# Adding the experts' output biases in the attention's projection, once per batch

## The chip, the cores and the metric

The kernel runs on one core of a Trainium2 chip. Its time is the device time of one execution in microseconds, the median of several runs. The engines of the core are TensorE (PE in the profile, with PEld for its weight loads), VectorE (DVE), ScalarE (ACT), GpSimd (POOL) and SyncE (SP), which here only issues DMAs.

## What is computed

Two layers on 16 x 256 tokens of width 128. Cut to what matters here:

```python
# layer 0
xn = layernorm(x)
attn = causal_linear_attention(xn) @ Wo.T              # 16 heads of 8
probs = softmax(xn @ Wg + bg)                          # 8 experts
selected = top2(probs) / (sum of the two + 1e-8)       # the gates
h = gelu(einsum('bsf,efh->bseh', xn, W1) + b1)
expert_out = einsum('bseh,ehf->bsef', h, W2) + b2      # b2: 8 x 128
x = x + attn + einsum('bsef,bse->bsf', expert_out, selected)
# layer 1
xn = layernorm(x)
x = x + (linear_attention(xn) @ w_proj + b_proj) + channel_mix(xn)
```

## The kernel before

The 4096 tokens lie in 32 tiles of 128; two tiles are a batch, four a group (8 groups). The stages, in the order of time:

- **First stage (to about 33 us).** For each group g: DVE takes the moments, POOL the deviation, ACT `normalise(g)` (L306) writes xn, PE transposes it (L335), ACT copies the transpose (L378), PE projects to values (L352) and queries and keys (L364), DVE multiplies by cosine and sine (L393). Four xn buffers take turns, so `normalise(4)` may only overwrite xn[0] once SP's DMA `save(0)` (L1281) has put it into DRAM. In ACT's order it is: values copy of g, xT copy of g+1, `normalise(g+2)`.
- **Routing (to about 58 us).** DVE picks two experts for each token, and the tokens are sorted by expert into 71 slots of 128 rows. Small products on PE and idle fillers (`keep_warm`, L320) run beside it.
- **Expert stage (to about 270 us).** PE's program is a fixed list of steps, one for each slot j: transpose the gathered tokens of slot j+2 (L545), `up` of slot j+1 (four f32 products, two records each, L561), what the list puts between, and `down` of slot j (L572 and L574). Between them stand the attention's parts: 32 cumulative sums (L700, L701; one every 2 slots or a little more), and for each batch two transposes (L746) and the projection (L776). PE executes strictly in this order. DVE does the elementwise part of the attention: tile (b, r) is apply (L712), outer (L667), sums (L721), and after r = 1 reciprocal, divide (L734), low part (L684) and phi (L642). ACT does gelu, copies and the high parts (L678). POOL gathers tokens and expert rows.
- **Second layer (to the end).** Linear attention and channel mix, group by group, the tokens' last additions done by DVE.

Before the change the bias b2 enters at each slot. It is split into three bf16 parts (POOL, L401 to L409), which six DMAs of SP (L1304) lay into three rows of `bias3`, zero elsewhere; a product of an all-ones matrix with the expert's 128 columns (L572) opens each `down`, with the column picked by a register. b_proj is added in the same manner (L1055, L1139).

SP's program order around the change is: loads of x, weights, `bg` (L1272), b2 (L1273), b_proj (L1274), mu (L1275, L1276), then `save(0)`, `save(1)`, two weight loads, then save and w2 loads in turn. A DMA waits in this queue for all that stand ahead of it.

```python
        if g >= NB:
            if layer == 0:
                act.wait_ge(xT_ps, g - NB + 2)
                act.wait_ge(xn_saved[n], g // NB * 16)
```

Of the kernel before, what the change touches and what calls it, by code (L numbers as in the profile page):

```python
# [22 lines left out]
BIASP, NBIAS = NE * D, NE * D + D  # L23
# [4 lines left out]
for _name, _n in (("ident", P), ("head_mask", P + H), ("cos", 2 * DH), ("sin", 2 * DH), ("first", NE),  # L28
                  ("row_no", 1), ("rows_in_front", 1), ("token_by_tile", NT),
                  ("ones", P), ("tri_incl", P), ("tri_excl", P), ("iota", P), ("token", NT * TOPK)):  # L30
    CONSTS[_name] = (_at, _at + _n)
    _at += _n
# [3 lines left out]
def constant_table():  # L36
# [21 lines left out]
    put("row_no", row)  # L58
    put("rows_in_front", P * row)
# [6 lines left out]
def build(nc, x_in, Wq, Wk, Wv, Wo, Wg, bg, W1, b1, W2, b2, w_qkv, w_proj, b_proj, W_r, W_k, W_v,  # L66
# [33 lines left out]
    xn = [sbuf(f"xn{p}", [P, GT, D]) for p in range(NB)]  # L100
# [18 lines left out]
    bias_sp = sbuf("bias_sp", [P, NBIAS // P])  # L119
    bias_rest = sbuf("bias_rest", [P, 2, NBIAS // P])  # L120
    bias_part = sbuf("bias_part", [P, 3, NBIAS // P], bf16)
    bias3 = sbuf("bias3", [P, NBIAS], bf16)
# [97 lines left out]
    y_tok, yT0 = sbuf("y_tok", [P, 2 * D])[:, :], sbuf("yT0", [P, 2 * P])[:, :]  # L220

# [9 lines left out]
    bias_in, bias_split, bias_rows = sem("bias_in"), sem("bias_split"), sem("bias_rows")  # L231
    small_ready, pool_const, warmed, bias_zero = sem("small_ready"), sem("pool_const"), sem("warmed"), sem("bias_zero")
# [164 lines left out]
    def split_biases(pool):  # L397


        pool.wait_ge(bias_in, 16 * 5)  # L400
        nc.gpsimd.tensor_copy(bias_part[:, 0, :], bias_sp[:, :]).then_inc(bias_split, 1)  # L401
        pool.wait_ge(bias_split, 1)
        nc.gpsimd.tensor_tensor(bias_rest[:, 0, :], bias_sp[:, :], bias_part[:, 0, :], ALU.subtract).then_inc(bias_split, 1)
        pool.wait_ge(bias_split, 2)
        nc.gpsimd.tensor_copy(bias_part[:, 1, :], bias_rest[:, 0, :]).then_inc(bias_split, 1)
        pool.wait_ge(bias_split, 3)
        nc.gpsimd.tensor_tensor(bias_rest[:, 1, :], bias_rest[:, 0, :], bias_part[:, 1, :], ALU.subtract).then_inc(bias_split, 1)
        pool.wait_ge(bias_split, 4)
        nc.gpsimd.tensor_copy(bias_part[:, 2, :], bias_rest[:, 1, :]).then_inc(bias_split, 1)  # L409
# [155 lines left out]
    def down(pe, base, s, e):  # L565
        j, p = slot(base, s), s % 2
        pe.wait_ge(gelu_ready, j + 1)
        if not from_(j, 1):
            pe.wait_ge(w2_in, 16 * NE)
            pe.wait_ge(bias_rows, 16 * 6)  # L570
# [169 lines left out]
    Y_COLS = slice(P, 3 * P)  # L740

    def attn_transpose(pe, b):

        pe.wait_ge(y_ready, b + 1)
        for t in range(2):
# [3 lines left out]
    def attn_yT(act, b):  # L749
# [3 lines left out]
        nc.scalar.copy(yT0, ps[6][:, Y_COLS]).then_inc(yT_ready, 1)  # L753
# [17 lines left out]
    def attn_project(pe, b):  # L771

        pe.wait_ge(tokens_put, b + 1)
        pe.wait_ge(yT_ready, b + 1)
        for t in range(2):
# [345 lines left out]
    def last_tensor(pe):  # L1121
# [16 lines left out]
        for h in range(2):  # L1138
            nc.tensor.matmul(out_half(h), ones_bf[:, :], bias3[:, BIASP:BIASP + D].unsqueeze(1).broadcast_to([P, HALF, D]),  # L1139
# [113 lines left out]
    with nc.Block() as block:  # L1253
        @block.sync
        def _(sp):
# [17 lines left out]
            sp.dma_start(bias_sp[:, 0:BIASP // P], b2.rearrange("e h -> (e h)").rearrange("(p c) -> p c", p=P)).then_inc(bias_in, 16)  # L1273
# [522 lines left out]
```

## Time and profile before

| | |
|---|---|
| median of 3 runs | 354.57 us (354.26 to 354.77) |
| the profiled execution | 354.33 us |
| its span, first to last instruction | 352.5 us |
| mean granted TensorE clock | 0.995 |
| instructions | 9136 |

Times of the views are microseconds from the start of the span. The span is 1.8 us shorter than the execution's own time. Records of PE overlap: a product's duration includes its drain, and its price in a dense stream is the distance to the next start. PEclk is the granted clock in tenths of full speed.

### The profile page before, as it was taken

The page shows a single profiled execution, that of the slowest core. Times are in us where ns is not written, and L with a number is a line of the kernel's source. Part 1 is how long each engine was busy: PE and PEld are TensorE (multiplying, and loading weights), DVE is VectorE, ACT ScalarE, POOL GpSimd, SP SyncE. Part 2 cuts the span into 40 slices and gives each one's busy share as a digit, 9 for nine tenths or more (in the row PEclk, how much of TensorE's full clock was granted, in tenths as well). Part 3 has the DMA queues.
Part 4 walks back from the last instruction along what each step waited for, and adds up shares of the span by engine and source line. Part 5 has one row for each costly group of instructions (what it writes and reads, how often), then busy time and mean ns, then how long its engine had stood idle before and what let it go on. Part 6 is the DMA issues. An engine that isn't in the chain of part 4 may idle for free.

```text
span 352.5 us, 9136 instructions
## 1 busy us (share of the span) xinstructions
PE 339.4 (96%) x2488; PEld 296.4 (84%) x2488; DVE 320.9 (91%) x633; ACT 271.4 (77%) x764; POOL 208.8 (59%) x229
## 2 busy tenths in 40 slices
PE   8999878999999999999999999999999899999995
PEld 3888334799999999999999899999998688778875
DVE  5999999899999999998899899998978799998665
ACT  2997946968887878787787678778985987777751
POOL 3899202843323666766776678778877278884110
PEclk9999989999999999999999999999999999999999
DMA  5896196454444555555555654565452002221112
GB/s 161 238 278 181 32 387 240 114 147 131 136 130 137 156 152 149 159 150 156 155 157 154 168 155 133 164 186 145 120 141 75 9 7 54 60 63 30 30 32 60
DMA packets 45520, 46.98 MB, mean 133 GB/s; under 512 B 6928, under 2 KB 33712, under 8 KB 45216
## 3 DMA queue, kind: packets, MB, share of 16 engines
q1 hardware_dynamic: 40432, 37.17, 35.7%
q0 software_dynamic: 4320, 8.86, 10.1%
q10 hardware_dynamic: 720, 0.38, 0.5%
q8 instruction: 22, 0.36, 0.5%
q14 instruction: 26, 0.21, 0.2%
HBM read 32.88 MB, written 13.50 MB: 132 GB/s over the span
## 4 chain that ended last, share of the span: by engine, by line
PE 86%; DVE 9%; DMA 2%; issue 2%; POOL 0%; ACT 0%; DVEq 0%; POOLq 0%
PE banks L574 18%; PE banks L561 18%; PE banks L700 7%; PE banks L701 7%; PE banks L364 4%; PE banks L1012 3%; PE banks L545 3%; PE banks L1041 2%; PE banks L1088 2%; PE banks L352 2%; PE banks L1070 2%; PE banks L1050 2%; PE banks L776 2%; PE banks L1022 2%; PE banks L1058 2%; PE banks L320 2%
## 5 line engine op out<-in xcount | busy, mean ns | idle before, releaser
L489 POOL DMA_INDIRECT xg<-xn_rows,slot_tok x71 | 76.5, 1077 | 77.0 <-PE banks L545 43.6
L591 ACT ACTIVATE xT<-banks,b1T 128x128 f32<-128x128 f32 x284 | 81.5, 375 | 18.8 <-PE banks L561 18.6
L506 POOL DMA_INDIRECT qk_exp<-expert_rows,ranki x64 | 74.0, 1156 | 19.1 <-issue 18.7
L574 PE MATMUL banks<-w_sb,xT 128*128 x568 | 78.9, 282 | 0.0
L561 PE MATMUL banks<-xgT,w 128*128 128x128 f32 x568 | 75.4, 276 | 0.0
L574 PEld LDWEIGHTS banks<-w_sb,xT 128*128 128x128 f32 x568 | 69.3, 192 | 0.5
L561 PEld LDWEIGHTS banks<-xgT,w 128*128 128x128 f32 x568 | 69.0, 192 | 0.8 <-issue 0.5
L712 DVE TENSOR_TENSOR cq<-banks,phi 128x360 f32<-128x360 f32 (+1 forms) x96 | 47.4, 548 | 7.6 <-PE banks L701 6.7
L684 DVE TENSOR_TENSOR low<-outer,high 128x1152 fp32r<-128x1152 f32 x32 | 43.5, 1358 | 3.2 <-ACT high L678 3.2
L721 DVE TENSOR_REDUCE sums<-cq 128x144 f32<-128x1152 f32 x32 | 43.0, 1343 | 0.1
L678 ACT CAST high<-outer 128x1152 fp32r<-128x1152 f32 x32 | 36.9, 1154 | 7.0 <-DVE outer L667 5.7
L667 DVE TENSOR_TENSOR outer<-phi,qkv 128x1024 f32<-128x1024 f32 x32 | 38.8, 1215 | 0.0
L700 PE MATMUL banks<-high,tri_r 128*128 128x360 f32 (+1 forms) x96 | 35.0, 365 | 0.0
L701 PE MATMUL banks<-low,tri_r 128*128 128x360 f32 (+1 forms) x96 | 32.3, 337 | 0.0
L600 ACT COPY ye<-banks 128x128 f32<-128x128 f32 x71 | 18.8, 265 | 13.0 <-PE banks L574 12.5
L320 PE MATMUL banks<-zeros_bf 128*128 128x512 bf16 x96 | 27.2, 427 | 1.0 <-DVE zeros_bf L1555 1.0
L306 ACT ACTIVATE xn<-x_sb,shift,rstd 128x128 f32<-128x128 f32 x60 | 24.9, 485 | 0.1
L963 POOL TENSOR_TENSOR outer<-outer,x_sb 128x512 f32<-128x512 f32 x7 | 8.9, 1276 | 22.0 <-DVE outer L958 22.0
L545 PE MATMUL banks<-cst,xg 128*128 128x128 f32 x71 | 19.6, 276 | 1.3 <-issue 0.5
L583 ACT COPY xgT<-banks 128x128 f32<-128x128 f32 x71 | 19.4, 273 | 0.8
L320 PEld LDWEIGHTS banks<-zeros_bf 128*128 128x128 bf16 x96 | 10.0, 111 | 11.6 <-issue 4.4
L287 POOL TENSOR_TENSOR rstd<-ve,mhalf 128x4 f32<-128x4 f32 x16 | 18.8, 1173 | 1.3
(210 smaller groups left out, 691.0 us busy)
## 6 DMA issues: line engine op xcount, KB each, us to landing
w<-in_L_ffn_W SPq DMA_DIRECT2D x71, 256.0 KB
expert_rows<-ye SPq DMA_DIRECT2D x71, 64.0 KB
expert_rows<-x_sb SPq DMA_DIRECT2D x2, 2048.0 KB, 9.7
x_sb<-in_L_attn_x SPq DMA_DIRECT2D x8, 256.0 KB, 4.0
xn_rows<-xn SPq DMA_DIRECT2D x8, 256.0 KB, 2.9
w_sb<-in_L_ffn_W SPq DMA_DIRECT2D x8, 256.0 KB, 3.9
out<-outer SPq DMA_DIRECT2D x7, 256.0 KB, 2.4
xg<-xn_rows,slot_tok POOLq DMA_INDIRECT x71
```

The costliest lines, as they stand in the source:

```text
L320: nc.tensor.matmul(ps[bank], zeros_bf[:, :], zeros_bf[:, :].unsqueeze(1).broadcast_to([P, 4, P]), start=True, stop=True)
L489: pool.indirect_dma_start(out=xg[n][:, :], out_offset=None, in_=xn_dram, in_offset=bass.IndirectOffsetOnAxis(ap=slot_tok[:, j:j + 1], axis ...
L506: pool.indirect_dma_start(out=y_moe[:, i, k, :], out_offset=None, in_=y_dram, in_offset=bass.IndirectOffsetOnAxis(ap=ranki[:, 0, k, i:i + ...
L561: last = nc.tensor.matmul(slot_bank(j)[:, c * P:(c + 1) * P], w1[n][:, c * P:(c + 1) * P], xgT[p][:, :], start=True, stop=True)
L574: last = nc.tensor.matmul(y, hidT[p][:, c, :], w2_sb[:, ds(e * NC + c, 1), :], start=False, stop=(c == NC - 1))
L591: last = nc.scalar.activation(hidT[p][:, c, :], slot_bank(j)[:, c * P:(c + 1) * P], ACT.Gelu_apprx_tanh, bias=b1T[:, ds(e * NC + c, 1)])
L667: nc.vector.tensor_tensor(outer_of(r)[:, :, 0:DH, :], k.unsqueeze(2).broadcast_to([P, H, DH, DH]), vv.unsqueeze(3).broadcast_to([P, H, DH, ...
L684: nc.vector.tensor_tensor(low[n], outer[r], high[n].bitcast(f32), ALU.subtract).then_inc(low_ready, 1)
L700: nc.tensor.matmul(o, w[:, :], high[at][:, cols], start=(m == 0), stop=False)
L701: last = nc.tensor.matmul(o, w[:, :], low[at][:, cols], start=False, stop=(m == len(parts) - 1))
L712: last = nc.vector.tensor_tensor(cq4[:, lo:hi, :, :], ps[n][:, 0:(hi - lo) * E9 * DH].rearrange("p (h e d) -> p h e d", e=E9, d=DH), q[:, ...
L721: nc.vector.tensor_reduce(sums[:, r, :, :], cq4, AX.X, ALU.add).then_inc(sums_ready, 1)
```

## The change

The sum over a token's two experts of gate times bias is a product of the token's eight gates (zero for the others) with the 8 x 128 matrix b2. The changed kernel adds it on PE where a batch's attention is projected, accumulated in the same PSUM bank: one fp32r product for each batch of two tiles, with 64 contraction rows and 256 columns. The 64 rows are the 16 gates (two tiles of eight experts) in a high and a low part, against the bias in a high and a low part. The product of each slot (L572) goes.

What it needs: the bias matrix in 128 rows, loaded by 16 small DMAs of b2 (8 rows each) and two of b_proj (1 row each) on SP's queue, behind the mu loads and ahead of the saves, after a wait for a memset; its parts by one operation on ACT and one on POOL in place of POOL's five and SP's six bias DMAs; the gates of all tokens by expert, from DVE operations in the routing and in `gates`; `split_gates` on DVE after tile (0, 1), two operations of 512 columns, the second of which waits for the first; one transpose on PE for every second batch, in front of the attention's own, where the first waits for `split_gates`; and one copy on ACT for each of them. b_proj uses the new matrix with an fp32r product.

```diff
-        nc.tensor.matmul(y, ones_bf[:, :], bias3[:, ds(e * D, D)], start=True, stop=False)
         for c in range(NC):
             last = nc.tensor.matmul(y, hidT[p][:, c, :], w2_sb[:, ds(e * NC + c, 1), :],
-                                    start=False, stop=(c == NC - 1))
+                                    start=(c == 0), stop=(c == NC - 1))
...
     def attn_transpose(pe, b):
         pe.wait_ge(y_ready, b + 1)
+        if b == 0:
+            pe.wait_ge(gates_split, 1)
+        if b % 2 == 0:
+            nc.tensor.transpose(ps[6][:, 3 * P:4 * P], gate_row[:, b * NGR:(b + 2) * NGR], ident)
...
+        if b % 2 == 0:
+            nc.scalar.copy(gT[:, :], ps[6][:, 3 * P:4 * P])
+        nc.scalar.copy(yT0, ps[6][:, P:3 * P]).then_inc(yT_ready, 1)
...
         for t in range(2):
-            last = nc.tensor.matmul(ps[5][:, t * D:(t + 1) * D], yT0[:, t * P:(t + 1) * P], wT[:, 0, :],
-                                    start=False, stop=True, skip_group_check=True)
-        last.then_inc(o_ps, 1)
+            nc.tensor.matmul(ps[5][:, t * D:(t + 1) * D], yT0[:, t * P:(t + 1) * P], wT[:, 0, :],
+                             start=False, stop=False, skip_group_check=True)
+        rows = slice(b % 2 * NGR, (b % 2 + 1) * NGR)
+        nc.tensor.matmul(ps[5][:, 0:2 * D], gT[rows, :], bias[rows, 0:2 * D], start=False, stop=True,
+                         skip_group_check=True).then_inc(o_ps, 1)
...
-        nc.tensor.matmul(ps[4], ones_bf[:, :], bias3[:, BIASP:BIASP + D].unsqueeze(1).broadcast_to([P, GT, D]),
+        nc.tensor.matmul(ps[4], ones_r[:, :], bias[:, BIASP:NBIAS].unsqueeze(1).broadcast_to([P, GT, D]),
...
-            sp.dma_start(bias_sp[:, 0:BIASP // P], b2.rearrange("e h -> (e h)").rearrange("(p c) -> p c", p=P)).then_inc(bias_in, 16)
-            sp.dma_start(bias_sp[:, BIASP // P:NBIAS // P], b_proj.rearrange("(p c) -> p c", p=P)).then_inc(bias_in, 16)
             sp.dma_start(mu[:, 0:1], mu_r.rearrange("(p c) -> p c", p=P)).then_inc(bias_in, 16)
             sp.dma_start(mu[:, 1:2], mu_k.rearrange("(p c) -> p c", p=P)).then_inc(bias_in, 16)
+
+            sp.wait_ge(zeros_ready, 2)
+            for q in range(P // (2 * NE)):
+                for t in range(2):
+                    lo = (2 * q + t) * NE
+                    sp.dma_start(bias_raw[lo:lo + NE, t * D:(t + 1) * D], b2).then_inc(bias_loaded, 16)
+            for lo in (0, 32):
+                sp.dma_start(bias_raw[lo:lo + 1, BIASP:NBIAS], b_proj.rearrange("(a c) -> a c", a=1)
+                             ).then_inc(bias_loaded, 16)
...
+    def bias_high(act):
+        act.wait_ge(bias_loaded, 16 * 18)
+        nc.scalar.activation(bias_high_of, bias_raw, ACT.Copy, scale=const("low_row")).then_inc(bias_ready, 1)
+
+    def bias_parts(pool):
+        pool.wait_ge(bias_ready, 1)
+        nc.gpsimd.tensor_tensor(bias[:, :], bias_raw, bias_high_of.bitcast(f32), ALU.subtract).then_inc(bias_ready, 1)
...
+            both = TT(oh[:, 0, :, :], oh[:, 0, :, :], oh[:, 1, :, :], ALU.add)
...
+            done(TT(gate_of_all, masked, oh[:, 0, :, :], ALU.mult))
...
+                done(TT(gate_of_all, gate_of_all, sel[0][:, :].unsqueeze(2).broadcast_to([P, NT, NE]), ALU.mult))
+
+            def split_gates():
+                whole = yT0[:, 0:NT * NE].rearrange("p (b f) -> p b f", b=B).unsqueeze(2).broadcast_to([P, B, 2, 2 * NE])
+                done(nc.vector.tensor_copy(gate_parts[:, :, :, 0, :], whole))
+                TT(gate_parts[:, :, :, 1, :], whole, gate_parts[:, :, :, 0, :].bitcast(f32), ALU.subtract
+                   ).then_inc(gates_split, 1)
...
                     tile(b, r, b % 2)
+                    if b == 0 and r == 1:
+                        split_gates()
```

## Rows read from the trace of the kernel before

**Rows 1.** The page: busy us (share of the span), instructions.
```profile
PE 339.4 (96%) x2488; PEld 296.4 (84%) x2488; DVE 320.9 (91%) x633; ACT 271.4 (77%) x764; POOL 208.8 (59%) x229
```

**Rows 2.** Busy time by window: engines, granted clock, DMA share, GB/s.
```profile
20.00:30.00 10.00, 10.00 (x63) 8.55 (x62) 9.97 (x23) 8.87 (x25) 9.53 (x14) 1.00 0.80 236
40.00:50.00 10.00, 6.58 (x26) 2.78 (x27) 9.38 (x30) 5.77 (x7) 0.00 (x0) 0.84 0.70 248
150.00:160.00 10.00, 10.00 (x82) 9.58 (x81) 9.84 (x14) 8.40 (x28) 5.80 (x6) 1.00 0.52 154
```

**Rows 3.** The chain that ended last, expert stage: start us, us, what.
```profile
157.80 0.16 PE banks L700
...
158.71 0.20 PE banks L701
158.91 0.07 PE banks L572
158.98 0.95 PE banks L574 x8
...
160.03 0.89 PE banks L561 x8
```

**Rows 4.** DVE's timeline, waits for PE: start us, us, what, idle before.
```profile
166.39 1.49 DVE L712 TENSOR_TENSOR cq<-banks,phi 128x360 f32<-128x360 f32 x3 [0.78 <-PE banks L701]
...
265.70 1.49 DVE L712 TENSOR_TENSOR cq<-banks,phi 128x360 f32<-128x360 f32 x3 [2.98 <-PE banks L701]
```

**Rows 5.** ACT's timeline, first stage.
```profile
17.79 0.59 ACT L378 COPY xT<-banks 128x512 f32<-128x512 f32 x1
18.27 1.65 ACT L306 ACTIVATE xn<-x_sb,shift,rstd 128x128 f32<-128x128 f32 x4
...
21.44 1.65 ACT L306 ACTIVATE xn<-x_sb,shift,rstd 128x128 f32<-128x128 f32 x4
```

**Rows 6.** SP's timeline, then the issues of lines 1281 and 1304, ns.
```profile
13.30 0.44 SPq L1273 DMA_DIRECT2D bias_sp<-in_L_ffn_b  x1
...
15.21 0.98 SPq L1281 DMA_DIRECT2D xn_rows<-xn  x2
...
L1281 SPq DMA_DIRECT2D xn_rows<-xn x8: 366/442/584, 15.2 to 29.9; - x8
DMA to landing us min/median/max: 2.2/2.9/5.7
...
L1304 SPq DMA_DIRECT2D bias<-bias_part x6: 562/601/1467, 37.8 to 41.9; - x6
```

**Rows 7.** PE's timeline: the transposes of groups 4 and 6.
```profile
20.32 0.60 PE L335 MATMUL banks<-cst,xn 128*128 128x128 f32 x4
...
26.84 0.60 PE L335 MATMUL banks<-cst,xn 128*128 128x128 f32 x4
```

**Rows 8.** PE's one long gap, the chain behind it, and ACT's wait.
```profile
46.69 0.56 PE L472 MATMUL banks<-by_turn,ones_r 128*128 128x72 f32 x2 [3.42 <-DVE by_turn L1656]
...
47.25 2.56 PE banks L320 x6
...
49.91 0.28 ACT L1382 CAST slot_no<-banks 128x144 f16<-128x144 f32 x1 [4.13 <-PE banks L477]
```

**Rows 9.** DVE at phi(2), and the chain's piece of PE's first L746.
```profile
81.67 0.68 DVE L642 SCALAR_TENSOR_TENSOR phi<-qk_exp,qkv 128x512 f32<-128x512 f32 x1
82.28 1.48 DVE L712 TENSOR_TENSOR cq<-banks,phi 128x360 f32<-128x360 f32 x3
...
81.86 0.22 PE banks L746 x2
```

**Rows 10.** The chain's first product of line 574 behind line 572.
```profile
152.19 0.17 PE banks L574
```

**Rows 11.** PE's timeline around the 32-row transposition.
```profile
34.04 0.60 PE L1504 MATMUL banks<-cst,outer 128*128 128x128 f32 x4
34.57 0.24 PE L1505 MATMUL banks<-cst,outer 32*128 32x32 f32 x1
34.75 2.98 PE L320 MATMUL banks<-zeros_bf 128*128 128x512 bf16 x13
```

More of the change, by code:

```diff
@@ L22 @@
 BIG = 3.0e38
-BIASP, NBIAS = NE * D, NE * D + D
+BIASP, NBIAS = 2 * D, 3 * D
+NGR = 4 * 2 * NE
 CONSTS = {}
@@ L58, in constant_table @@
     put("row_no", row)
+    put("low_row", row // 32 % 2)
     put("rows_in_front", P * row)
@@ L99, in build @@
     NB = 4
-    xn = [sbuf(f"xn{p}", [P, GT, D]) for p in range(NB)]
+    xn_all = sbuf("xn_all", [P, NB, GT, D])
+    xn = [xn_all[:, p, :, :] for p in range(NB)]
     xT = [sbuf(f"xT{p}", [P, GT, P]) for p in range(2)]
@@ L118, in build @@
     bg_sb = sbuf("bg_sb", [P, NE])
[L119 to L122, printed above, removed]
+    bias = sbuf("bias", [P, NBIAS], f32r)
     ones_bf = sbuf("ones_bf", [P, P], bf16)
@@ L220, in build @@
     y_tok, yT0 = sbuf("y_tok", [P, 2 * D])[:, :], sbuf("yT0", [P, 2 * P])[:, :]
+    gT = sbuf("gT", [P, P], f32r)
+    bias_high_of = high[2][:, 0:NBIAS]
+    bias_raw = phi_all[:, 4 * D:4 * D + NBIAS]
+    gate_row = xn_all[:, 2:4, :, :].rearrange("p n c f -> p (n c f)")
+    gate_parts = gate_row.bitcast(f32r).rearrange("p (b c s f) -> p b c s f", b=B, c=2, s=2)
+    gate_of_all = yT0[:, 0:NT * NE].rearrange("p (a e) -> p a e", e=NE)
     ps_all = st.enter_context(nc.psum_tensor("banks", [P, 8 * 512], f32))
@@ L1138, in last_tensor @@
         for h in range(2):
-            nc.tensor.matmul(out_half(h), ones_bf[:, :], bias3[:, BIASP:BIASP + D].unsqueeze(1).broadcast_to([P, HALF, D]),
+            nc.tensor.matmul(out_half(h), ones_r[:, :], bias[:, BIASP:NBIAS].unsqueeze(1).broadcast_to([P, HALF, D]),
                              start=True, stop=False, skip_group_check=True)
@@ L1299, in _ @@
                 sp.wait_ge(x_loaded[g], 16)
-            sp.wait_ge(bias_split, 5)
-            sp.wait_ge(bias_zero, 1)
-            for n in range(3):
-                for lo, hi in ((0, BIASP), (BIASP, NBIAS)):
-                    sp.dma_start(bias3[n:n + 1, lo:hi].rearrange("a (p c) -> a p c", p=P),
-                                 bias_part[:, n, lo // P:hi // P]).then_inc(bias_rows, 16)
             rows = y_dram.rearrange("(p r) d -> p (r d)", p=P)
@@ L1377, in _ @@
             nc.scalar.copy(b1T[:, :], ps[1][:, 0:NE * NC]).then_inc(w_late_ready, 1)
+            bias_high(act)
             for g in range(1, NG - 2):
@@ L1428, in first @@
                 act.wait_ge(pool_const, 4)
+                act.wait_ge(bias_ready, 2)
                 nc.scalar.activation(scrap["scalar"], scrap["zero"], ACT.Gelu_apprx_tanh).then_inc(warmed, 1)
@@ L1457, in _ @@
                     deviation(pool, 0, g + 5, g + 5)
-            split_biases(pool)
+            bias_parts(pool)
             pool.wait_ge(logits_read, 1)
@@ L1555, in _ @@
             nc.vector.memset(zeros_bf[:, :], 0.0).then_inc(zeros_ready, 1)
-            nc.vector.memset(bias3[:, :], 0.0).then_inc(bias_zero, 1)
+            nc.vector.memset(bias_raw, 0.0).then_inc(zeros_ready, 1)
             nc.vector.memset(keep, 1.0).then_inc(route, 1)
@@ L1583, in choose @@
                 v.wait_ge(v_raw, NT // 2)
-                v.wait_ge(bias_in, 16 * 5)
+                v.wait_ge(bias_in, 16 * 3)
                 TT(lg, qkv3[:, :, 3 * D:NQ], per_expert(bg_sb[:, :]), ALU.add).then_inc(logits_read, 1)
@@ L1719, in _ @@
                 rope_sum_vector(v, NG - 1, f)
+            both = TT(oh[:, 0, :, :], oh[:, 0, :, :], oh[:, 1, :, :], ALU.add)
+            n_route[0] += 1
+            both.then_inc(route, 1)
             v.wait_ge(gate_exp, 1)
-            done(RED(row(5), masked, AX.X, ALU.add))
+            RED(row(5), masked, AX.X, ALU.add)
+            v.wait_ge(route, n_route[0])
+            done(TT(gate_of_all, masked, oh[:, 0, :, :], ALU.mult))
             def gates():
@@ L1747, in _ @@
             for b in range(2):
+                if b == 1:
+                    v.wait_ge(bias_ready, 2)
                 phi(v, b, b)
```

22 lines of the change are left out of this document (5 added, 17 removed).

## The prediction

> **What bounds the kernel now.** I read the page first. TensorE (PE) is busy in 96% of the span and VectorE (DVE) in 91% [rows 1], so neither share alone says which one sets the end. The windows say more. In the first stage (20 to 30 us) PE and DVE are both full; from 150 to 160 us, inside the expert stage, PE is full and DVE has 0.16 us of idle in ten [rows 2]. The chain that ended last, asked for a stretch of the expert stage, runs on PE alone [rows 3]: what PE issues there is on the path, and the pieces of the chain are the true price of an instruction (start to start), where its own duration includes a drain that the next one hides. The DVE timeline gives the second limit: its apply (L712) waited for PE in few places, the first large one 0.78 us at 166.39, the largest the last, 2.98 us at 265.70 [rows 4]; they lie where the schedule puts extra slots. So DVE follows PE closely, but it follows.
>
> The first stage has the same form. The chain there is PE's transposes and projections at 3.17 us for each group of four tiles, and ACT's order (values copy, xT copy, normalise) has the same period: normalise starts at 18.27 and at 21.44 us [rows 5]. SP is not busy in any table, but its queue issues loads back to back there [rows 6], and that is the part of the profile that decides this change.
>
> **The change on SP's queue.** 18 loads (16 copies of b2 by eight rows, two of b_proj) stand between the mu loads and the first save of xn. Two loads (L1273, L1274) go. Four issues from 13.30 to 15.21 us give 0.478 us each [rows 6]; so the first save moves by 16 x 0.478 = 7.6 us, from 15.21 to 22.8. The new wait in front of them, on a memset at DVE's start, is long over by 15 us and costs nothing. Who waits behind it: save(0) must land before normalise(4) may overwrite xn[0]. Its landing takes 2.2 at best, 2.9 us in the median [rows 6]. Today that is 17.4 to 18.1 us and normalise(4) starts at 18.27, as soon as ACT is free [rows 5]: the cover is under a microsecond. After: 22.8 + 2.2 to 2.9 = 25.0 to 25.7, so ACT stands for 6.7 to 7.4 us; I take 7.1. PE needs these tiles for the transposes at 20.32 [rows 7], 0.4 us behind ACT, and ACT, PE and DVE hold the rest of their work behind it. Nothing catches up, as PE and ACT both run at 3.17 us a group with no gap; only about 0.2 us comes back that PE lost to DVE between the transposes at 20.32 and 26.84, two groups in 6.52 us where 6.34 would do [rows 7]. Save(1) to save(3) follow at once and are in time. Bounds for one issue: 0.37 (the shortest save, 366 ns) to 0.6 (the median of L1304, 601 ns) [rows 6], that is 5.9 to 9.6 us for 16, and a stall of about 5.0 to 9.4.
>
> **The clock.** PE will then idle for some 6.8 us. The trace shows one such gap: PE waited 3.42 us for DVE (L472), and the six warm-up products behind it took 2.56 us on the chain (47.25 to 49.81), where 13 of the kind took 2.98 (0.22 each, 1.3 for six) [rows 8, 11]; the window's granted clock is 0.84, the lower level of 1.2 GHz for part of it [rows 2]. So a gap costs about 1.3 us in these rows and 0.2 in L472; I take 1.4, with 0 and 3 as bounds. It is on the path, because the work behind this gap is real.
>
> The Trainium skill (TensorE: Matmul & The Clock Gate, Why this matters for your kernels) warns against idle gaps of TensorE between bursts of products, since the clock falls behind them; the trace agrees, with the 0.84 just given.
>
> **SP and the others between 33 and 60 us.** The five Pool splits, the six bias DMAs (3.6 us by six medians of L1304 [rows 6]) and SP's wait for them go; the fill of expert_rows starts earlier. DVE's chain of routing sets the time there and none of this stands in it, so I count 0. ACT's bias_high (about 0.45 us, 384 columns, by the xT copy's 0.59 for 512 [rows 5]) lies in front of the 4.13 us that ACT idles before L1382 [rows 8]; Pool's subtraction, one in place of five, before its long wait for the slots. DVE's three or four extra routing operations come after the slot numbers have left, 256 columns each, some 0.4 us by phi's 0.68 for 512 [rows 9]; they delay phi and the first low part by some 0.7 us, and PE's first cumulative sum by about 0.5. That is absorbed by the next item.
>
> **A new wait of PE at the gates.** split_gates stands behind tile (0,1) and phi(2) on DVE, which end at 82.28 [rows 9]. It is two operations on 512 columns, one of which needs the other's end: 0.68 us each by phi (L642, 512 columns) [rows 9], so ready at about 83.7. PE's first transpose of the attention (L746) starts at 81.86 now [rows 9] and would wait in order, with up and down of the next slots behind it. With the gates' own transpose (0.11) L746 starts at 83.85: +1.95 us on PE, whatever it had saved before. DVE itself is 1.35 later and keeps its slack (the waits of [rows 4] are still ahead of it), so it doesn't become the bound.
>
> **What PE saves.** Per slot the bias product L572 costs 0.07 us of the chain behind a cumulative sum [rows 3] and little less elsewhere. The eight products behind it cost 0.95, where the eight of L561 cost 0.89 [rows 3]: the first of them takes 0.17, not 0.11 [rows 10], because its weights can't load behind so short a product. I take both as gone: 0.06 + 0.06 = 0.12 a slot. Behind the gates' wait 65 slots are left: 7.8 us (3.9 if only the product itself counts).
>
> **What PE gets.** Seven more transposes at 0.11 (two of L746 take 0.22 [rows 9]): 0.8 us. 16 products of 64 rows by 256 columns, fp32r: 360 columns cost 0.16 and 432 cost 0.20 [rows 3], so 0.12 for 256, or 1.9 us. But they use half of the array's rows. The trace has one operation on part of the rows, the transposition L1505 of 32 rows: it starts 0.20 us after the last of L1504 (34.57 against 34.04 + 3 x 0.11) and the product behind it 0.18 later, where whole-array neighbours are 0.11 and at most 0.11 apart [rows 11]. So entering and leaving costs 0.1 each: 0.32 a product, 5.1 us in all. Bounds: 0.12 (1.9 us) and 0.45, if both sides cost the full 0.165 by which one transposition exceeds its step (four of L1504 take 0.60, so one takes 0.27) (7.2 us). I take 5.1, because the 32-row transposition is the nearest row.
>
> The Trainium skill (TensorEngine Tiling (Array Packing), Key Properties) says that a change of tiling mode drains TensorE. By that rule every one of the 16 products pays twice; the row of L1505 agrees in kind, and without the rule and the row the sum would be 3.2 us lower. The tail's bias products (L1055, L1139) change from bf16 to fp32r with the same columns: 0.
>
> **Sum.** 7.1 (stall) + 1.4 (clock) - 0.2 + 1.95 (gates) - 7.8 + 0.8 + 5.1 = +8.35 us. On the profiled execution's 354.33 this is 362.7; the median of the runs is 0.24 higher, so 362.9.
>
> **Rivals.** (1) The stall as above, but the 64-row products slip in at the price of their columns: 3.2 us less, 359.7. For it: L1505 is one row, of another shape and type; against it: no other row shows part of the rows used. (2) The first stage doesn't wait: small loads of eight rows are issued so fast that save(0) still lands by 18.3. Then only the expert stage counts: +0.05 with the dear products (354.6), -3.15 with the cheap ones: 351.4, faster. To be faster by 0.7 us even with cheap products, the stall must stay under 2.45 us; with 0.2 to 0.9 us of cover that is 3.4 us at most for 16 issues, 0.21 each, and the shortest issue of these rows is 0.37 [rows 6]. (3) An issue costs 0.6, as the bias DMAs of L1304 did: a stall of 9.4, 365.2. (4) The bias product saves 0.06 only: +3.9, 366.8; the 0.17 of [rows 10] speaks against it.
>
> **Chances.** Forecast 0.50, rival 1 0.28, rival 2 0.05 (0.03 of it faster), rival 3 0.10, rival 4 0.07. A measurement of this kernel tells 0.2% (0.7 us) from no change. Faster 0.04, the same 0.02, slower 0.94. Range: 357.5 (rival 1 with the best landing and no clock loss: 354.3 + 6.7 - 3.4) to 366.5 (rival 3 with the forecast's other terms and somewhat more clock loss).
>
> **What would show it.** Right: SP's issues of the saves start near 22.8; ACT's normalise (L306) has one idle of about 7 us ended by the save; PE a gap of about 7 us near 20.5 and a granted clock under 1 behind it; DVE's choice of experts starts some 8 us later; L746's first start is about 2 us late relative to the first slot; the first product of L574 takes 0.11; the 64-row products show 0.3 between neighbours. It is wrong if the small loads are issued much faster than 0.47, or if ACT is not held at normalise(4).

## The result and the profile after

The changed kernel takes 365.77 us (median of 6 runs, 364.65 to 367.82), the kernel before 354.69 (354.26 to 356.19) beside it: a ratio of 1.0305 with an interval of 1.0269 to 1.0342. It is slower, inside the predicted range (357.5 to 366.5) and 2.9 us above the forecast of 362.9. The profiled execution took 365.91, its span is 364.1 against 352.5: 11.6 us, which this section places. Every ratio here is formed from the fast executions of both kernels alone, so it can differ from the quotient of the two medians.

The page of the changed kernel, its busy shares and its chain that ended last:

```profile
PE 342.7 (94%) x2441; PEld 302.6 (83%) x2441; DVE 321.1 (88%) x638; ACT 272.0 (75%) x773; POOL 210.0 (58%) x225
...
PE 79%; DVE 11%; SPq 4%; issue 2%; DMA 2%; ACT 1%; ACTq 1%; DVEq 0%
```

PE has 47 instructions fewer than in [rows 1] and is busy 3.3 us longer. SP's queue, a queue of DMA issues, holds 4% of the chain.

The first place, SP's timeline and ACT's and PE's behind it (start us, us, instruction, idle before it):

```profile
14.86 5.46 SPq L1291 DMA_DIRECT2D phi<-in_L_ffn_b  x16
20.36 0.55 SPq L1293 DMA_DIRECT2D phi<-in_L_attn_b_proj  x2
20.96 0.95 SPq L1299 DMA_DIRECT2D xn_rows<-xn_all  x2
...
23.26 1.65 ACT L315 ACTIVATE xn_all<-x_sb,shift,rstd 128x128 f32<-128x128 f32 x4 [4.69 <-DMA xn_rows<-xn_all]
...
24.96 1.12 PE L344 MATMUL banks<-cst,xn_all 128*128 128x128 f32 x4 [4.28 <-ACT xn_all L315]
```

The 16 loads take 5.46 us from the first to behind the last, 0.34 each, so save(0) is issued at 20.96 where it was 15.21 [rows 6]. It has landed at 23.26, 2.3 us later, and ACT, which normalised at 18.27 before [rows 5], has stood 4.69 us for it. PE stood behind ACT and then ran on the lower clock: the next row has a granted clock of 0.54, where four transposes and four products take 2.6 us (24.96 to 27.57) for 1.3 before (20.32 to 21.62). Windows of PE's stretch behind the gap, then of the stretches behind the second place below (PE, PEld, DVE, ACT, POOL, clock, DMA share, GB/s):

```profile
24.96:28.36 3.40, 3.40 (x13) 3.04 (x14) 0.54 (x1) 2.96 (x9) 3.16 (x6) 0.54 0.93 265
...
88.40:91.80 3.40, 2.94 (x17) 2.97 (x18) 3.40 (x6) 1.51 (x7) 0.07 (x1) 0.66 0.25 81
91.80:95.20 3.40, 3.40 (x22) 3.15 (x22) 2.06 (x2) 3.28 (x11) 0.94 (x1) 0.84 0.37 109
```

At the end of the first stage (PE's last four transposes, L1504 before and L1516 after) PE is at 39.98 against 34.04: +5.94. The stall is 4.69 of it, the other 1.25 are the clock less what came back between the groups: PE's whole step for this group took 3.79 us (24.96 to 28.75) where it took 2.30 (20.32 to 22.62), so the clock cost 1.49 there.

The routing gives 0.81 of it back: the slots' table, which all gathers wait for, is written on DVE at 62.66 against 57.53, +5.13. This is DVE's timeline in the changed kernel, and below it that of the kernel before for the same two operations and the reduction ahead of them:

```profile
39.84 0.42 DVE L1605 TENSOR_TENSOR cq<-outer,r 128x256 f32<-128x256 f32 x1
40.30 0.42 DVE L1606 SCALAR_TENSOR_TENSOR outer<-cq,cst 128x256 f32<-128x256 f32 x1
...
42.59 0.82 DVE L1605 TENSOR_TENSOR outer<-cq,r 128x256 f32<-128x256 f32 x1
```

```profile
33.45 0.42 DVE L1592 TENSOR_REDUCE r<-outer 128x32 f32<-128x256 f32 x1
33.90 0.93 DVE L1593 TENSOR_TENSOR cq<-outer,r 128x256 f32<-128x256 f32 x1
34.87 1.38 DVE L1594 SCALAR_TENSOR_TENSOR outer<-cq,cst 128x256 f32<-128x256 f32 x1
```

Before, Pool worked beside them: sums of the rope up to 35.96 and the five splits of the bias up to 37.67. In the changed kernel Pool is idle from 38.15 to 42.12, and only the operation at 42.59, beside Pool's one subtraction, takes longer again. Run 1 below keeps the five splits and gains the same 0.81: its choice of experts starts 6.24 us late (39.23 for 32.99) and its table 5.43 late (62.96). There Pool ends at 39.75, before DVE's two operations at 40.18 and 40.64, which take 0.43 each. So the gain comes with the delay of the stage and not with the change of Pool's work.

The second place is PE's first transpose of the gates, on DVE's timeline and PE's:

```profile
87.57 0.42 DVE L1755 CAST xn_all<-yT 128x512 fp32r<-128x512 f32 x1
88.02 0.69 DVE L1756 TENSOR_TENSOR xn_all<-yT,xn_all 128x512 fp32r<-128x512 f32 x1
...
88.86 0.30 PE L749 MATMUL banks<-cst,xn_all 128*128 128x128 f32 x1 [2.02 <-DVE xn_all L1756]
89.00 0.38 PE L751 MATMUL banks<-cst,y_tok 128*128 128x128 f32 x2
89.22 1.65 PE L566 MATMUL banks<-xgT,w 128*128 128x128 f32 x8
90.66 1.92 PE L577 MATMUL banks<-w_sb,xT 128*128 x8
```

PE stands 2.02 us; the attention's transposes start on the chain at 89.16 where L746 stood at 81.86 [rows 9], +7.30. Of that 5.13 is the routing's start, 2.17 the gates. And the price goes on: eight products of L566 take 1.49 on the chain and eight of L577 1.71, where they cost 0.89 each [rows 3], and the nine behind them 0.21 and 1.01 where they cost 0.11 and 0.89. The granted clock is 0.66 and 0.84 in the windows above.

The third place is the steady part. The chain that ended last (start us, us, what):

```profile
142.04 0.45 PE banks L785 x4
142.49 0.31 PE banks L788
142.80 0.36 PE banks L703
143.16 0.16 PE banks L704
143.32 0.17 PE banks L703
...
145.11 0.89 PE banks L577 x8
146.00 0.11 PE banks L550
146.11 0.89 PE banks L566 x8
```

The slot without its bias product saves what was predicted: 0.07 + 0.95 [rows 3] has become 0.89. The 64-row product (L788) costs 0.31 itself and makes the sum behind it 0.36 where whole-array neighbours take 0.17: 0.50 in all.

DVE's apply of each tile (L712, now L715) gives a ruler over the expert stage. Its start, after less before, in us:

| tile of the order | 0 | 1 | 2 | 3 | 9 | 15 | 21 | 31 |
|---|---|---|---|---|---|---|---|---|
| after less before | 4.95 | 5.36 | 6.35 | 9.34 | 9.79 | 10.12 | 10.68 | 11.63 |

So 9.3 of the 11.6 us are there by the fourth tile, and the 28 steps behind it add 2.3.

### The profile page after: what moved, and what is told of

Read it like the earlier page. It is cut to its first block, busy times and chain, and to the rows that moved or that the text cites. A ratio compares the mean times of both kernels' runs of the same rounds, so it can differ in the third digit from the quotient of the medians.

```text
span 364.1 us, 8993 instructions
## 1 busy us (share of the span) xinstructions
PE 342.7 (94%) x2441; PEld 302.6 (83%) x2441; DVE 321.1 (88%) x638; ACT 272.0 (75%) x773; POOL 210.0 (58%) x225
## 4 chain that ended last, share of the span: by engine, by line
PE 79%; DVE 11%; SPq 4%; issue 2%; DMA 2%; ACT 1%; ACTq 1%; DVEq 0%
PE banks L566 16%; PE banks L577 16%; PE banks L703 8%; PE banks L704 7%; PE banks L1023 3%; PE banks L373 2%; PE banks L329 2%; PE banks L550 2%; PE banks L1099 2%; PE banks L1052 2%; PE banks L1081 2%; PE banks L1061 2%; PE banks L785 2%; PE banks L1033 2%; PE banks L1069 2%
## 5 line engine op out<-in xcount | busy, mean ns | idle before, releaser
L494 POOL DMA_INDIRECT xg<-xn_rows,slot_tok x71 | 78.3, 1103 | 80.1 <-PE banks L550 47.3
L511 POOL DMA_INDIRECT qk_exp<-expert_rows,ranki x64 | 74.8, 1168 | 19.5 <-issue 18.9
L566 PE MATMUL banks<-xgT,w 128*128 128x128 f32 x568 | 76.2, 277 | 0.2 <-ACT xgT L586 0.2
L577 PE MATMUL banks<-w_sb,xT 128*128 x568 | 76.1, 277 | 0.1
L577 PEld LDWEIGHTS banks<-w_sb,xT 128*128 128x128 f32 x568 | 72.3, 193 | 0.7 <-issue 0.3
L566 PEld LDWEIGHTS banks<-xgT,w 128*128 128x128 f32 x568 | 69.7, 193 | 0.7 <-issue 0.7
L715 DVE TENSOR_TENSOR cq<-banks,phi 128x360 f32<-128x360 f32 (+1 forms) x96 | 47.3, 548 | 13.0 <-PE banks L704 13.0
L704 PE MATMUL banks<-low,tri_r 128*128 128x360 f32 (+1 forms) x96 | 32.3, 337 | 0.0
L315 ACT ACTIVATE xn_all<-x_sb,shift,rstd 128x128 f32<-128x128 f32 x60 | 24.9, 485 | 4.7 <-DMA xn_rows<-xn_all 4.7
L329 PE MATMUL banks<-zeros_bf 128*128 128x512 bf16 x96 | 26.3, 416 | 1.0 <-DVE zeros_bf L1567 1.0
L703 PEld LDWEIGHTS banks<-high,tri_r 128*128 128x128 f32 x96 | 18.1, 188 | 2.7 <-DVE low L687 0.8
```

What stands on the lines that cost most here:

```text
L494: pool.indirect_dma_start(out=xg[n][:, :], out_offset=None, in_=xn_dram, in_offset=bass.IndirectOffsetOnAxis(ap=slot_tok[:, j:j + 1], axis ...
L511: pool.indirect_dma_start(out=y_moe[:, i, k, :], out_offset=None, in_=y_dram, in_offset=bass.IndirectOffsetOnAxis(ap=ranki[:, 0, k, i:i + ...
L566: last = nc.tensor.matmul(slot_bank(j)[:, c * P:(c + 1) * P], w1[n][:, c * P:(c + 1) * P], xgT[p][:, :], start=True, stop=True)
L703: nc.tensor.matmul(o, w[:, :], high[at][:, cols], start=(m == 0), stop=False)
L704: last = nc.tensor.matmul(o, w[:, :], low[at][:, cols], start=False, stop=(m == len(parts) - 1))
L715: last = nc.vector.tensor_tensor(cq4[:, lo:hi, :, :], ps[n][:, 0:(hi - lo) * E9 * DH].rearrange("p (h e d) -> p h e d", e=E9, d=DH), q[:, ...
```

## The experiments

Each was run beside the kernel before. The first eight ran on two chips on which every kernel, the one before too, takes 25 to 29 us longer (medians of the kernel before 379.93 and 383.48), in short waits of all engines that begin at about 120 us; up to there their traces agree with the others, so for these I use the ratio and the ruler up to tile 9 (at 128.9 us in run 1), always against the trace of before shown here. In runs 3 and 8 the first of these waits lies between tiles 8 and 9. The last four ran beside a kernel before of 354.87.

**1. The loads alone.** The kernel before, with 16 more loads of b2 into a tile that nobody reads, in front of save(0):

```diff
+            for q in range(16):
+                sp.dma_start(extra[NE * q:NE * (q + 1), :], b2)
```

> The kernel before with 16 more loads of b2 (8 rows each, into a tile that nobody reads) between the mu loads and the first save, nothing else. My account: save(0) moves by 16 times the 0.34 us that these loads took in the changed kernel, 5.5 us; normalise(4) idles about 4.7 us for the save, PE's gap is followed by the lower clock, and the end comes 5 us later or a little less: about 359.7, ratio 1.014. Rival (the first stage's delay is made up by the routing, whose chain is DVE's): under 1.5 us, 356. Rival (the whole slowdown is on SP's queue): 365.8.

Measured: 385.49 against 379.93, 1.0132 (1.0077 to 1.0187). The ruler stands at +5.54 on every tile from 0 to 9. ACT's timeline:

```profile
23.38 1.65 ACT L307 ACTIVATE xn<-x_sb,shift,rstd 128x128 f32<-128x128 f32 x4 [4.81 <-DMA xn_rows<-xn]
```

So the issue of the loads, and nothing else of the change, holds the first stage. Rival 2 falls: the small loads do hold save(0) up.

**2. All of the change, its 18 loads later.** They go behind the save and the weight load of group 3:

```diff
             for g in range(2, NG):
                 save(g)
                 load_w2(g - 2)
+                if g == 3:
+                    load_bias()
```

> The changed kernel with the 18 bias loads behind the save and w2 load of group 3, where no one waits for the saves that follow. My account: normalise(4) has no idle for a save, the slot numbers are ready near 57.5 us as before the change, and the end is 5 us earlier than the changed kernel's: about 360.7, ratio to before 1.017. What is left (6 us) is the gates' wait with its clock and the 64-row products. Rival (stall hidden anyway): 365.8. Rival (stall is all): 354.7.

Measured: 384.06, 1.0055 (1.0007 to 1.0103), run together with run 1; the ratio of 1.017 that was expected is missed. No idle before ACT's normalise is left, and the ruler begins at 1.08. But in the changed kernel it jumps by 4.39 from tile 0 to tile 3, across the gates, and here by 2.25 (to 3.33). The wait is the same, and what follows it isn't. PE's timeline, and below it the windows around it:

```profile
84.49 0.30 PE L749 MATMUL banks<-cst,xn_all 128*128 128x128 f32 x1 [2.02 <-DVE xn_all L1759]
84.63 0.38 PE L751 MATMUL banks<-cst,y_tok 128*128 128x128 f32 x2
84.85 1.06 PE L566 MATMUL banks<-xgT,w 128*128 128x128 f32 x8
```

```profile
80.80:84.20 3.40, 1.67 (x13) 1.43 (x11) 3.33 (x6) 1.96 (x8) 1.35 (x1) 1.00 0.37 118
84.20:87.60 3.40, 3.11 (x28) 3.14 (x29) 3.40 (x6) 2.20 (x9) 0.42 (x1) 1.00 0.27 85
```

Here the clock stayed at its full level behind the same gap, and the products take their 1.06 of the timeline rather than 1.65 and 1.92.

**3. The slot's bias product alone.** The kernel before without L572 (the biases of the experts' outputs are left out); the first product of the slot starts the accumulation.

```diff
-        nc.tensor.matmul(y, ones_bf[:, :], bias3[:, ds(e * D, D)], start=True, stop=False)
```

> The kernel before without the bias product of each slot (the experts' output biases are left out of the result). It measures the saving by itself. My account: 71 times 0.12 us on PE's chain, 8.5 us, of which DVE, which then has nearly no slack in the steps of two slots, may keep back one or two: 346.2 to 348, ratio 0.976 to 0.982. Rival (only the product's own 0.06 counts): 4.3 us, 350.4. Rival (DVE is the bound, it gets back only its hidden 0.2 us a batch): 3 us, 351.5.

Measured: 374.52, 0.9869 (0.9824 to 0.9915), run with 1 and 2, so about 5.0 us and not the 6.7 to 8.5 that were expected. It is repeated as run 9.

**4. The gates' gap filled.** The changed kernel, with 32 short products of zeros into the part of a bank that the gates' transpose writes afterwards, in front of PE's wait for the gates:

```diff
         if b == 0:
+            for _ in range(32):
+                nc.tensor.matmul(ps[6][:, 3 * P:4 * P], zeros_bf[:, :], zeros_bf[:, :], start=True, stop=True)
             pe.wait_ge(gates_split, 1)
```

> The changed kernel with 32 idle products of 128 columns on PE ahead of its wait for the gates. They fill 1.8 of the 2.2 us that PE waits there. My account: the clock then stays up, and up(7) and down(6) behind the wait take 0.89 us each in place of 1.49 and 1.71: 1.5 us less, about 364.3. Rival (the products behind the wait are slow for another reason, a drain or a late gather): no change, 365.8.

Measured: 388.79, 1.0157 (1.0093 to 1.022). PE's timeline, and below it a window:

```profile
86.55 1.95 PE L748 MATMUL banks<-zeros_bf 128*128 128x128 bf16 x32
88.64 0.33 PE L751 MATMUL banks<-cst,xn_all 128*128 128x128 f32 x1
...
89.02 1.06 PE L566 MATMUL banks<-xgT,w 128*128 128x128 f32 x8
```

```profile
90.80:94.20 3.40, 3.40 (x25) 3.15 (x24) 2.93 (x3) 3.32 (x12) 0.94 (x1) 1.00 0.36 114
```

The wait's end is nearly where it was (88.64 against 88.86); PE is busy with nothing useful until then, and the clock stays at 1.00. The ruler at tile 3 shows 7.51 in place of 9.34. Of these 1.83 us 0.14 are there already at tile 2, ahead of the gap; from tile 2 to tile 3 it rises by 1.3 where it rose by 3.0, so 1.7 us of the changed kernel were the clock behind the gates' gap.

**5. Run 2 again,** as the ground for the next three.

> The kernel of e2 again (changed kernel, the 18 loads behind the fourth save), on another chip if there is one, as the base of the next three. By the traces of e2 up to 130 us (3.8 us behind the kernel before at the tenth apply, and 0.2 more every two batches): 5.5 us slower than before at the end, 360.2, ratio 1.016. Rival (what I saw of e2 after 135 us is of the kernel, not of that chip): 378.

Measured: 389.37, 1.0139 (1.0032 to 1.0246). The same kernel with the same gap now loses the clock: L749 waits 2.01, the windows behind it have 0.62 and 0.88, eight products of L566 take 1.91, and the ruler reaches 5.01 at tile 3 where run 2 reached 3.33. Between the two executions lie 1.68 us at one place, and the clock is all that I see to differ there. The profiled execution of run 5 is its longest, 394.16; but the changed kernel's, an ordinary one of 365.91, has the same rise of 3.0 us from tile 2 to tile 3.

**6. The product over all 128 rows.** Two tiles of gates, each with the other batch's half set to zero, in place of 64 rows of one tile; else as run 5.

```diff
+            for n in range(2):
+                half = slice(n * NGR, (n + 1) * NGR)
+                nc.scalar.copy(gT[n][half, :], ps[6][half, 3 * P:4 * P])
...
-        nc.tensor.matmul(ps[5][:, 0:2 * D], gT[rows, :], bias[rows, 0:2 * D], start=False, stop=True,
+        nc.tensor.matmul(ps[5][:, 0:2 * D], gT[b % 2][:, :], bias[:, 0:2 * D], start=False, stop=True,
```

> e5 with the gates' product over all 128 contraction rows: two gate tiles, in each of which the half of the other batch is zero (two memsets at the start, one more ACT copy for each pair of batches). Same sums. My account (entering and leaving the 64-row form costs 0.38 us of the 0.50 that a product costs): the product takes 0.12 and its successor 0.17, 16 times 0.38 is 6.1 us on PE, of which DVE may keep back up to 2: 354.2 to 356. Rival (the cost is of the fp32r product with 256 columns, or of its place behind the projection, not of its rows): 360.

Measured: 384.55, 1.002 (0.9974 to 1.0067). PE's timeline (starts and durations):

```profile
112.80 0.61 PE L787 MATMUL banks<-wT,yT 128*128 128x128 f32 x4
113.17 0.36 PE L789 MATMUL banks<-bias,gT 128*128 128x256 f32 x1
113.37 0.33 PE L703 MATMUL banks<-high,tri_r 128*128 128x360 f32 x1
113.53 0.32 PE L704 MATMUL banks<-low,tri_r 128*128 128x360 f32 x1
```

From the projection's start to L704 it is 0.73 us; in the changed kernel it is 1.12 (142.04 to 143.16 above). The same columns over twice the rows save 0.39 at each of 16 products, 6.2 us. The ruler falls from tile 3 to 9 (4.56 to 4.05), where that of run 5 rises (5.01 to 5.47).

**7. `split_gates` one tile earlier.** As run 5, with `if b == 0 and r == 0: split_gates()`.

> e5 with split_gates one tile earlier, behind tile (0,0) in place of tile (0,1). The split then lies in a stretch in which DVE is late anyway. My account: PE's wait of 2.0 us at the first gates' transpose goes, and DVE's 1.1 us stay on the path: 1 to 2 us less than e5, 358.5. Rival (DVE is the bound there, it makes no difference where the 1.1 us lie): 360.2, as e5.

Measured: 385.72, 1.0146 (1.0093 to 1.02): by the ratio nothing against run 5 (1.0139), on the chip where both intervals are wide. In the trace PE no longer waits for the gates, the clock stays up, and the ruler is at 3.05 at tile 3 and 3.13 at tile 9, where run 5 has 5.01 and 5.47 and run 2 3.33 and 3.79. But this trace starts its expert stage later, for a reason that is not in the edit. PE's long gap in the routing is the same (3.40 us, in run 5 3.41), and from its end to the slots' table run 7 takes 12.03 us where run 5 takes 10.77. The windows around the stretch behind that gap, of run 7 and then of run 5:

```profile
50.00:55.00 5.00, 5.00 (x39) 2.20 (x38) 3.49 (x12) 2.48 (x10) 0.00 (x0) 0.66 0.29 93
```

```profile
50.00:55.00 5.00, 4.89 (x50) 2.32 (x48) 4.77 (x15) 3.47 (x14) 0.00 (x0) 0.93 0.40 109
```

So the ruler has to be read from the table on. With that, the edit gives 3.2 us against run 5, which lost the clock at the gates, and 1.6 against run 2, which didn't. At tile 1 the ruler less the table's delay is 1.3 (run 5: 0.2): DVE's two operations (0.42 and 0.69) now stand in front of that tile, at the stage's start, where DVE has no lead, and they stay on the path as was expected. By the same reading the change of run 6 is worth 0.4 at tile 3, which has one of its products ahead of it.

**8. All three mends,** runs 5, 6 and 7 together.

> e5 with both edits of e6 and e7. My account: 352.5 to 354.5, at or just under the kernel before (ratio 0.994 to 1.000): what the slot products give back is then held by DVE, which needs 11.7 us for a batch where PE needs 11.6. Rival (DVE does not bind): PE's chain gives -8.5 + 0.9 + 1.9 + 1.1, 350.

Measured: 382.51, 0.996 (0.9903 to 1.0017); the ruler is 3.21 at tile 3 and 2.45 at tile 8. Run 12 repeats it. The traces side by side, all in us later than the kernel before:

| | changed | run 2 | run 4 | run 5 | run 6 | run 7 | run 8 |
|---|---|---|---|---|---|---|---|
| slots' table | 5.1 | 0.8 | 5.0 | 0.8 | 2.3 | 2.0 | 2.2 |
| ruler at tile 3 | 9.3 | 3.3 | 7.5 | 5.0 | 4.6 | 3.1 | 3.2 |
| the second less the first | 4.2 | 2.6 | 2.5 | 4.2 | 2.2 | 1.0 | 1.0 |

The clock behind the gates' gap is the 1.6 to 1.7 between 4.2 and the next two values, and the gates' wait itself the 1.6 between 2.6 and 1.0.

**9. Run 3 again,** on a chip like the first.

> The kernel of e3 again (kernel before without the bias product of each slot; the biases of the experts' outputs are left out), as the base of the next two. In e3's trace DVE's apply came only 0.8 us early at the ninth tile, where PE had been relieved of some 16 products, 1.9 us. If DVE holds the rest, it is 4 to 6 us faster than before in all, ratio 0.983 to 0.989, since the places with extra slots still give PE's part. Rival (PE alone sets the end): 8.5 us, 0.976.

Measured: 349.86, 0.9862 (0.9837 to 0.9888). The ruler goes from +1.18 at tile 0 to −4.25 at tile 31: 5.4 us over the stage, where 71 slots at 0.12 would be 8.5. PE's timeline and the groups of L545 (the first product of a gathered slot) and DVE's L711 (the apply), with the idle before them, in a fence of their own:

```profile
193.64 0.30 PE L545 MATMUL banks<-cst,xg 128*128 128x128 f32 x1 [1.25 <-issue]
```

```profile
L711 DVE TENSOR_TENSOR cq<-banks,phi 128x360 f32<-128x360 f32 (+1 forms) x96 | 47.3, 548 | 5.1 <-PE banks L700 5.0
...
L545 PE MATMUL banks<-cst,xg 128*128 128x128 f32 x71 | 19.6, 276 | 4.0 <-issue 2.4 <-DMA xg<-xn_rows,slot_tok 1.5
```

In the kernel before PE is idle 1.3 us in front of L545 over all slots; here 4.0. So 3.1 us are missing, and PE waits 2.7 us more here. One of these waits is for a gather: 1.09 us at 66.55, ahead of the first tile. The four in the expert stage, 2.4 us, are not: the gather for the product at 193.64 had landed at 187.24. What this product waited for is ACT's copy of the slot before (L582), by the order of ACT's timeline:

```profile
192.06 1.15 ACT L677 CAST high<-outer 128x1152 fp32r<-128x1152 f32 x1 [1.00 <-DVE outer L666]
193.12 0.26 ACT L599 COPY ye<-banks 128x128 f32<-128x128 f32 x1
193.27 0.27 ACT L582 COPY xgT<-banks 128x128 f32<-128x128 f32 x1
```

In ACT's order the copy stands behind the attention's high part, which here waited 1.00 us for DVE's outer product. At each of the four places the copy ends 0.10 us before L545 starts, and at three of them the high part ends just ahead of the copies.

**10. and 11. DVE relieved.** In 10 the kernel before computes the low parts of only half of the state's columns (DVE's L684 on 576 of 1152; the other half of the low parts is zero). 11 does that in the kernel of run 9.

```diff
-        nc.vector.tensor_tensor(low[n], outer[r], high[n].bitcast(f32), ALU.subtract).then_inc(low_ready, 1)
+        nc.vector.tensor_tensor(low[n][:, 0:HED // 2], outer[r][:, 0:HED // 2], high[n][:, 0:HED // 2].bitcast(f32),
+                                ALU.subtract).then_inc(low_ready, 1)
```

> The kernel before with DVE's low parts (L684) on 576 of 1152 columns, the others zero from the start; the attention loses those low parts in its result. DVE is relieved of 0.6 us in each of 32 tiles, 19 us in all. My account (PE sets the end before the change): within 1 us of the kernel before, ratio 0.997 to 1.003, although DVE has 19 us less. Rival (DVE is a bound of equal rank already): several us faster, 0.985.

> Both edits, of e9 and e10 (leaves out the biases of the experts' outputs and half of the low parts). My account (DVE holds what e9 lacks): PE's full 8.5 us come through, less the half us of e10: ratio 0.975 to 0.977, some 3 us faster than e9. Rival (what e9 lacks is lost on PE itself or in the gathers): as e9.

Measured: 10 takes 353.88, 0.997 (0.9957 to 0.9983), 11 takes 348.49, 0.9837 (0.98 to 0.9874). The groups of DVE's apply, of run 10 and then of run 11:

```profile
L713 DVE TENSOR_TENSOR cq<-banks,phi 128x360 f32<-128x360 f32 (+1 forms) x96 | 47.4, 550 | 22.2 <-PE banks L702 22.2
```

```profile
L712 DVE TENSOR_TENSOR cq<-banks,phi 128x360 f32<-128x360 f32 (+1 forms) x96 | 47.4, 549 | 19.4 <-PE banks L701 19.4
```

DVE waits for PE 22.2 us in run 10 where it waited 6.7 before, and the kernel is only 1.0 us faster: before the change PE sets the end almost everywhere. Without the slot's product the same relief is worth 1.4 us by the medians (349.86 to 348.49), with overlapping intervals, and not the 3 us that were expected. The traces show a part of it at one place: ACT's high part waits 0.19 us for DVE there and not 1.00, and PE 0.45 (at 190.72) and not 1.25. So DVE, by way of ACT, keeps back 0.8 us of what PE gives at that step. Both edits together, 6.4 us, stay under the 8.5 of 71 slots; where the rest goes is open.

**12. Run 8 again,** beside 9 to 11.

> The kernel of e8 again. In e8's early trace the apply of tile 8 was 2.45 us behind the kernel before and it gained about 0.3 us for every batch until 150 us. So at the end 1.5 us slower to 1 us faster than before, ratio 0.996 to 1.004. Rival (the 2.45 us stay, DVE binds): 1.007.

Measured: 353.24 (352.32 to 354.69) against 354.87, 0.9947 (0.9929 to 0.9966). It is faster than both kernels, than the one before by 1.6 us (0.5%). Its chain at a projection (its profiled execution is the slowest of its four, 354.69):

```profile
144.98 0.45 PE banks L787 x4
145.43 0.12 PE banks L789
145.55 0.17 PE banks L703
145.71 0.18 PE banks L704
```

The product costs its 0.12 and nothing behind it. The ruler starts at 1.46, is 2.65 at tile 3 and falls to −1.12 at tile 31; in the changed kernel it rose by 2.29 over the same stretch. The difference of the two slopes is 6.06 us; 14 of the 16 products lie in this stretch, and the 0.39 of run 6 by 14 gives 5.5 of it. In this execution, too, the routing took longer behind its 3.4 us gap (11.85 us from there to the table, where the kernel before took 10.84).

## Why the prediction was right, and where it was off

Right in its sign, its range and its main mechanism, the stall at save(0). The forecast lies 2.9 us low, and that is the sum of errors that partly cancel: the stall was taken 2.4 us too long and the 64-row products 2.9 us too short, and with the measured stall alone the forecast would have been 360.5. That 365.77 still lies in the range is in part luck. The range left out one of its own rivals, rival 4 (366.8), and its lower end took a stall of 6.7 where the bound worked out was 5.0. Against the predicted 8.35:

| term | predicted | measured | from |
|---|---|---|---|
| stall of ACT at save(0) | 7.1 | 4.69 | ACT's idle, 4.81 in run 1 |
| clock behind it, less 0.2 | 1.2 | 1.25 | rest of +5.94 at the stage's end |
| routing | 0 | −0.81 | +5.13 at the slots' table |
| gates' wait | 1.95 | 2.17 | +7.30 less 5.13 |
| clock behind the gates | not counted | 1.42 | 1.49 + 1.71 for 2 x 0.89; 1.7 by run 4 |
| 65 slots | −7.8 | −7.8 | 0.12 each, 0.13 behind a cumulative sum |
| transposes of the gates | 0.8 | 0.8 | 7 x 0.11, the chain's piece at 138.93 |
| 64-row products | 5.1 | 8.0 | 16 x 0.50 |
| rest | 0 | about 1.9 | what is left of 11.6 |

**SP's queue, the mechanism right, the size off.** The step was "four issues from 13.30 to 15.21 us give 0.478 us each". The neighbours of the new loads do cost that; the 16 loads themselves cost 0.34 (5.46 us; a single one 288 to 379 ns), 0.14 less. The landing of save(0) took 2.3, at the lower end that was given. Rival 3 (0.6 an issue) falls with it. 16 issues at 0.34 are below the shorter of my two bounds, 5.9 us, and the stall of 4.69 below its bound of 5.0; by the prediction's own sign (issued much faster than 0.47) this size was missed.

**The clock behind the first gap** came as worked out from L472's gap, 1.25 for 1.2, with a granted clock of 0.54 behind it: 1.49 at the group itself, of which about 0.2 came back, as foreseen.

**The gates' wait** came as predicted, behind the same two operations (0.42 and 0.69, where 0.68 was taken for each; the gates' transpose took 0.30 on the chain and not 0.11, which makes up for most of it). **The step that failed is that no price was put on the clock behind it.** I counted the first gap's clock and not this one's, though the row that I had priced it by, L472's, had a gap of 3.42 us. Run 4 shows it directly: with the gap filled and its end earlier by only 0.22, of which 0.14 were there before the gap, 1.7 us go behind it. Runs 2 and 5, one kernel, show that a gap of 2.0 us may or may not do it: 1.68 us between them. Run 6 has the gap too (2.01) and kept its clock. What decides it in one execution stays open. The Trainium skill (TensorE: Matmul & The Clock Gate, Why this matters for your kernels) warns of idle gaps between bursts of products; the traces here agree for 4.28 us, and for 2.0 in two of four executions (the changed kernel and run 5, not runs 2 and 6).

**The slots** came as predicted, both halves of it: the product's 0.06 and the 0.06 of the product behind it. Rival 4 falls. Alone, the removal is worth 5.0 us (run 9) and not 8.5: the place is right, and the schedule takes part of it back. Some steps are then shorter than the work of ACT for them, the high part (1.15 us) and the copies behind it, which itself follows DVE's outer product, and PE waits for ACT's copy (4.0 us of idle in front of L545 against 1.3, of which 1.1 for one gather). In the changed kernel this shows in the same form, 2.2 against 1.3, one wait of 1.05, behind a copy that ended at 206.10 and a high part that waited 0.79 for DVE:

```profile
206.20 0.30 PE L550 MATMUL banks<-cst,xg 128*128 128x128 f32 x1 [1.05 <-issue]
```

These 0.9 us are the half of the rest that I can name; 0.2 more are the clock behind the gates, at the nine products after the 16 counted in the table. The other 0.8 us I can't place.

**The 64-row products, the term that was mis-sized.** 0.32 was taken, with 0.45 as the upper bound, and 0.50 measured. The step was "entering and leaving costs 0.1 each", from a row with transposes around it. Measured, they cost 0.19 each: the product takes 0.31 where its columns cost 0.12, and the cumulative sum behind it 0.36 where it costs 0.17. Run 6 isolates it: only the number of rows changes, and 0.39 go at each. Rival 1 (the products at the price of their columns) falls for the same reason. The Trainium skill (TensorEngine Tiling (Array Packing), Key Properties) has the rule that changing the mode drains TensorE, without a price; here it is 0.39 us for one product between whole-array neighbours.

**The routing** was to be 0. It gained 0.8, from Pool's idleness beside DVE. That the two go together is read from rows (0.42 alone, 0.82 to 1.38 beside Pool). Run 1, with the delay and with the splits, gains the same 0.81, so it is the delay that brings it; no run took Pool's work away with DVE's left where it was.

The change's own saving (some 7.8 us) is thus real and on the path, though the schedule takes part of it back. What made the kernel slower is where its help was put: 4.7 + 1.25 for loads in front of a save that ACT needs, 2.2 + 1.4 for gates that come one tile late, 6.2 for using half of the rows. Run 12 mends these three and beats the kernel before by 1.6 us.

## What to carry to other kernels

A small load costs its queue not much less than a large one (here 0.34 to 0.48 us an issue, where the loads of w2, 256 KB each, took 0.51 to 0.69): before loads go into a queue, look for the DMA behind them that an engine waits for, and what cover that wait has. A product on part of the array's rows between whole-array ones costs its entry and exit (0.39 us); fill the rows with zeros instead. Price a wait in PE's stream twice, with and without the fall of the clock behind it, also where it is only 2 us. Where two traces are compared by the start of an operation, subtract first what they differ by ahead of the stage. And a wait that the profile puts down to nothing can be one for an engine that works in order and has a long operation in front of the short one that is needed.

## What the runs showed of the hardware that was not expected

- The same DVE operation on 128 x 256 fp32 elements takes 0.42 us with Pool idle, and 0.82, 0.93 and 1.38 beside Pool's operations (rows above); the reduction with one input (L1592), beside the same Pool work, keeps its 0.42. The Trainium skill (GPSIMD Engine Reference, Specifications) says that Pool shares its memory interface with VectorE, with contention for DVE instructions of two SBUF inputs; these rows agree in kind, though it doesn't befall each such instruction: one more with two inputs (L1585 at 32.99) took 0.42 beside Pool, while the same operation took 1.58, 1.55 and 1.35 beside it in runs 2, 9 and 12.
- A gap of 2.02 us on TensorE was followed by a granted clock of 0.66 in one execution and 0.62 in another, and by 1.00 in a third, which ran the same kernel as the second (2.01 against 2.02): a difference of 1.68 us on the path.
- The gap of 3.4 us that each of these kernels has on PE in the routing (3.38 to 3.43 us) didn't cost the same in each execution. From its end to the slots' table took 10.77 to 10.85 us in nine of the fourteen profiled executions, 11.85 to 12.10 in four (runs 6, 7, 8 and 12) and 10.29 in one (run 11), where the granted clock stayed at 1.00. If all of that is the clock's, one and the same gap cost 0, 0.5 to 0.6, or 1.6 to 1.8 us.
- Back-to-back issues of small loads by SP take 0.34 us each, where single issues of other tensors take 0.48 in the same stretch. In runs 2 and 12, where they lie between larger transfers, the 16 take 5.72 and 6.20 us (0.36 and 0.39 each).
